# Reading a unit's two PSUM score tiles with one maximum and one exp of 1024 columns in a two-layer attention and FFN kernel

## The reference

```python
x = L0_attn_x                                    # (16, 512, 128)
xn = _layernorm(x); x = x + attn0(xn) + ffn0(xn) # 16 heads of 64, causal, ALiBi slopes
xn = _layernorm(x)
# second attention (attn1), H = 8, D = 8
q1, q2 = q[..., 0, :], q[..., 1, :]              # after rotary; k the same
def sdpa(q, k, v):
    scores = jnp.einsum('bshd,bthd->bhst', q, k) * d ** (-0.25)
    w = jax.nn.softmax(scores, axis=-1)
    return jnp.einsum('bhst,bthd->bshd', w, v)
o = sdpa(q1, k1, vfull) - lam * sdpa(q2, k2, vfull)
o = (o * rsqrt(mean(o * o) + 1e-8) * ln_w + ln_b) * (1 - LAMBDA_INIT)
x = x + o.reshape(b, s, e) @ Wo.T + ffn1(xn)
```

## Time and profile before

| | |
|---|---|
| runs, us | 2466.5, 2472.6, 2473.2; median 2472.6 |
| profiled execution | 2475.1 us, its span on the engines 2473.2 us |
| mean granted TensorE clock | 0.982 |
| PE matmuls / DVE / ACT / POOL busy | 2349.1 / 1832.7 / 1876.5 / 1443.5 us |
| maxima L1362 | 1024, 679 ns each |
| exps L1044 | 1024, 607 ns each |

### The profile page before, as it was taken

One profiled execution on the slowest core, in us unless ns is written; L12 is line 12 of the kernel. 1 busy time (PEld: TensorE's weight loads), 2 busy tenths in 40 slices (PEclk: granted clock), 3 DMA queues, 4 the chain that ended last, 5 costly groups with the idle time before them and its releaser, 6 DMA issues.

```text
span 2473.2 us, 82166 instructions
## 1 busy us (share of the span) xinstructions
PE 2349.1 (95%) x32896; PEld 1136.1 (46%) x32896; DVE 1832.7 (74%) x5637; ACT 1876.5 (76%) x4707; POOL 1443.5 (58%) x1356
## 2 busy tenths in 40 slices
PE   6999999999999999999999999999999999999877
PEld 3554444444544444444444544444444444544322
DVE  5568687787877778687787877778786887877674
ACT  4877877877778787877878777887777877787434
POOL 5975574756648466574756657475574756556201
PEclk9999999999999999999999999999999999999877
DMA  3011020200202020020201102020020201102020
GB/s 100 4 38 23 7 58 3 57 6 20 45 3 62 3 57 8 6 58 3 62 3 29 36 7 57 3 57 7 7 58 3 62 2 40 25 3 57 2 56 5
DMA packets 59946, 70.45 MB, mean 28 GB/s; under 512 B 11056, under 2 KB 55344, under 8 KB 56368
## 3 DMA queue, kind: packets, MB, share of 16 engines
q1 hardware_dynamic: 59568, 65.21, 11.4%
HBM read 35.04 MB, written 29.36 MB: 26 GB/s over the span
## 4 chain that ended last, share of the span: by engine, by line
PE 77%; DVE 16%; ACT 3%; issue 2%; DMA 1%; SPq 0%; POOL 0%; POOLq 0%; DVEq 0%; ACTq 0%
PE pj L1595 18%; PE pj L1691 12%; PE sc L1659 10%; PE pj L1721 10%; PE sc L1676 5%; PE sc L1768 5%; PE pj L1707 5%; DVE mx L1362 5%; PE pj L1615 5%; PE sc L1754 4%; DVE pq L1309 4%; PE pj L1585 3%; ACT pt L1044 1%; DVE y L1330 1%; DVE onrm L1372 1%
## 5 line engine op out<-in xcount | busy, mean ns | idle before, releaser
L845 POOL TENSOR_SCALAR pq<-pq,rsum 128x128 f32<-128x128 f32 (+3 forms) x1024 | 1151.8, 1139 | 772.8 <-DVE rsum L1316 771.2
L1362 DVE TENSOR_REDUCE mx<-sc 128x1 f32<-128x512 f32 x1024 | 644.1, 679 | 247.5 <-PE sc L1768 247.1
L996 ACT ACTIVATE pq<-pq,mx 128x128 f32<-128x128 f32 (+3 forms) x1024 | 569.8, 570 | 25.9 <-DVE mx L1309 25.7
L1044 ACT ACTIVATE pt<-sc 128x512 f32<-128x512 f32 x1024 | 543.9, 607 | 36.0 <-PE sc L1754 34.6
L1309 DVE CUSTOM_DVE_ANT_0 pq<-sc,relkey 128x128 f32<-128x128 f32 (+3 forms) x1024 | 448.5, 484 | 158.7 <-PE sc L1659 156.1
L1014 ACT ACTIVATE pt<-sc 128x512 f32<-128x512 f32 (+1 forms) x768 | 376.6, 535 | 162.3 <-PE sc L1676 159.5
L1659 PE MATMUL sc<-K,Q 64*128 64x128 f32 (+3 forms) x2048 | 362.5, 452 | 15.7 <-DVE mx L1309 9.4
L1691 PE MATMUL pj<-pt,v 128*32 128x512 f32 (+3 forms) x4096 | 303.8, 437 | 8.5 <-DVE y L1330 5.7
L1676 PEld LDWEIGHTS sc<-ident,pq 64*128 64x128 f32 x5120 | 200.1, 138 | 189.8 <-issue 99.7
L1595 PE MATMUL pj<-xnT,wqkv 128*32 128x512 f32 x2048 | 263.1, 606 | 4.0 <-ACT xnT L947 2.0
L1676 PE MATMUL sc<-ident,pq 64*128 64x64 f32 x5120 | 234.6, 227 | 7.4 <-DVE mx L1309 4.0
(11 more groups left out here) (117 smaller groups left out, 2836.7 us busy)
## 6 DMA issues: line engine op xcount, KB each, us to landing
scr_p<-y SPq DMA_DIRECT2D x160, 128.0 KB, 2.4
QS<-scr_p SPq DMA_DIRECT2D x30, 384.0 KB, 5.8
KS<-scr_p SPq DMA_DIRECT2D x30, 384.0 KB, 8.5
x_in<-in_L_attn_x SPq DMA_DIRECT2D x16, 256.0 KB, 2.9
scr_p<-tanh SPq DMA_DIRECT2D x32, 128.0 KB, 2.4
out_x<-xres SPq DMA_DIRECT2D x15, 256.0 KB, 2.3
QS<-nrow SPq DMA_DIRECT2D x180, 4.0 KB
wqkv<-in_L_attn_w_qkv SPq DMA_DIRECT2D x1, 1536.0 KB, 6.5
```

The costliest lines, as they stand in the source:

```text
L845: pool.tensor_scalar(rows, rows, rsum[:, row_slot(i, p), c:c + 1], None, ALU.mult).then_inc(s_scl, 1)
L996: act.activation(rows, rows, ACT.Exp, scale=-1.0, bias=mx0[:, row_slot(i, p), c:c + 1], accum_out=lsum[:, row_slot(i, p), c:c + 1]).then_i ...
L1044: act.activation(pt1[:, 2 * (unit % UNITS) + h, :], sc[tile_bank(i, "st1", 2 * n + h)][:, :], ACT.Exp, scale=float(DS) ** -0.25).then_inc( ...
L1362: dve.reduce_max(mx1[:, g % 2, at:at + 1], sc[tile_bank(i, "mx1", 2 * t + h)][:, :], AXIS.X).then_inc(s_mxd1, 1)
```

## The change

The six score banks are allocated as three PSUM tensors of two neighbouring banks each, and `sc[n]` becomes a view of one half, so all other users stay as they are. `row_max1` waits once for both tiles and takes both maxima with one instruction over a 128x2x512 source, writing two columns of `mx1` that lie 8 apart; it adds 2 to its semaphore at its end. `exp1` waits once for both tiles and writes both slots of `pt1` with one instruction, adding 2. The numbers of matmuls, their order and every other step are the same.

```diff
-        sc = [ps(f"sc{n}") for n in range(SCB)]
+        sc_pairs = [ctx.enter_context(nc.psum_tensor(f"sc{n}", [P, 2, T], F32)) for n in range(SCB // 2)]
+        sc = [sc_pairs[n // 2][:, n % 2, :] for n in range(SCB)]
...
-                for h in range(2):
-                    act.wait_ge(s_st1, i.upto(L1N, 2 * n + h + 1))
-                    act.activation(pt1[:, 2 * (unit % UNITS) + h, :], sc[tile_bank(i, "st1", 2 * n + h)][:, :],
-                                   ACT.Exp, scale=float(DS) ** -0.25).then_inc(s_exp1, 1)
+                act.wait_ge(s_st1, i.upto(L1N, 2 * n + 2))
+                both = tile_bank(i, "st1", 2 * n)
+                assert both % 2 == 0 and tile_bank(i, "st1", 2 * n + 1) == both + 1
+                slot = 2 * (unit % UNITS)
+                act.activation(pt1[:, slot:slot + 2, :], sc_pairs[both // 2][:, :, :], ACT.Exp, scale=float(DS) ** -0.25).then_inc(s_exp1, 2)
...
-                for h in range(2):
-                    at = 2 * NT * h + n
-                    dve.wait_ge(s_mxf1, i.upto(L1N, 2 * t + h + 1))
-                    dve.reduce_max(mx1[:, g % 2, at:at + 1], sc[tile_bank(i, "mx1", 2 * t + h)][:, :], AXIS.X).then_inc(s_mxd1, 1)
+                dve.wait_ge(s_mxf1, i.upto(L1N, 2 * t + 2))
+                both = tile_bank(i, "mx1", 2 * t)
+                assert both % 2 == 0 and tile_bank(i, "mx1", 2 * t + 1) == both + 1
+                dve.reduce_max(mx1[:, g % 2, n:n + 2 * NT + 1:2 * NT], sc_pairs[both // 2][:, :, :], AXIS.X).then_inc(s_mxd1, 2)
```

## The result

| | before | after |
|---|---|---|
| median of 7 runs each, us | 2473.2 (2466.5 to 2481.9) | 2489.6 (2483.4 to 2490.8) |
| profiled execution / its span | 2475.1 / 2473.2 | 2489.4 / 2487.6 |
| distance from batch to batch, steady state | 147.46 | 148.08 |
| maximum / exp, ns each | 679 and 679 / 607 and 607 | 1217 / 1025 |

The kernel got slower: the ratio of the runs is 1.005, 95% interval 1.0034 to 1.0067, which is 8 to 17 us. The forecast was 2474.3 with a range up to 2485; it is outside. (One correction to the text ahead of it: a batch has 32 units, which are 64 tiles. No term of the sum uses the wrong number.)

A forecast was written before the change was run, and what follows sets the result against it. TensorE (PE), 97% busy, was taken to bound the kernel. Per period +2x0.26-0.33 = +0.19, 14 periods +2.7, tail -1.0: total +1.7 us, so the median 2472.6 becomes 2474.3; range 2463 to 2485, the forecast's own 2470 to 2480.

The forecast's parts named there:

- rivals 2 and 4: Wide instructions: 2, the whole start is saved, 2463 us, chance 0.10; 4, nothing is saved, 2485 us, chance 0.11.
- the sum of the whole start: With 0.15 and 0.18 us saved per pair: loss 28x0.10 = 2.8, gain 14x0.65 = 9.1, tail 3, giving 2463.
- The gains on the chain: Savings of wide maxima and exps that reach the chain in one steady-state period: 0.33 us together.
- term (b): DVE near 1426.7 to 1431.28 us: three maximum pairs' savings reach the chain, 0.21 less 0.01, so 0.20 us per period.
- Term (a): The maximum pair at 1323.66 us opens a DVE run on the chain lasting to 1330; saves 0.07 us per period.
- (c): The exp pair at 1445.33 us is on the chain and holds an L1754; saves 0.06 us per period.
- The pattern: Twice per period, 28 times, DVE starts pair two on a half-filled pair; after the change it starts 0.49 us later.
- PE loses 0.26: Per pattern, the k projection's weight loads wait for the residual sum L1285 and start at 1310.78 instead of 1310.52 us.
- rival 3: At DVE's pair two of the pattern, PE loses the full 0.42 us; tail adds 4; 2484 us, chance 0.13.
- its own signs: Forecast wrong if wide instructions last near 1.28 and 1.08, k projection starts on time, or period leaves 147.7 by over 0.3.
- The tail: Last two batches, behind about 2290 us: maxima save 1.2 and exps 0.9, late second tiles cost 1.1; total -1.0 us.
- late second tiles: In the tail, about ten starts wait for a second tile not yet filled, few on the chain; cost +1.1 us.

The follow-up runs named there:

- four units by tile: After, but the maxima of units 14, 15, 27 and 28 of each batch are read tile by tile; ratio to before 0.9978, period 147.09 us.
- maxima alone: Maxima wide as in after, exps tile by tile as in before; ratio to before 1.0056, period 148.09 us.
- the kernel that adds 1: After, but each wide maximum and exp adds 1 instead of 2 and waits count units; ratio to before 1.0034, period 147.84 us.
- joint wait: Before with narrow maxima, but DVE waits for both tiles before the first, banks released one by one; ratio to before 1.0069, period 148.42 us.
- four units by tile with adds of 1: After with units 14, 15, 27, 28 read tile by tile and adds of 1 instead of 2; ratio to before 0.9976, period 146.95 us.
- exps alone: Exps wide as in after, maxima tile by tile as in before; ratio to before 1.0004, period 147.46 us.
- joint release: Before with narrow maxima, but both banks are released by the second reduce, adding 1 per unit; ratio to before 1.0068, period 148.31 us.
- narrow adding 2: Before, but each narrow maximum adds 2 to its semaphore and thresholds are doubled; ratio to before 1.0015, period 147.60 us.

## Why the prediction was wrong, point by point

**What bounds the kernel: right.** PE is the bound, DVE and ACT have slack, and neither's saved busy time came out as such: DVE's fell by 29 us and ACT's by 22.5 over the span. That PE's would stay the same was wrong, it fell by 42 with the matmuls side by side and the kernel still got slower.

**The sizes of the wide instructions: right.** 1217 and 1025 ns against 1.21 and 1.02 us; rivals 2 and 4 (whole start saved, nothing saved) fall with them. (The 0.65 in the sum of the whole start isn't worked out there; the three terms at 0.15 and 0.18 add up to at most 0.78, which would make it 2461. The forecast doesn't use it.) In a run of two, DVE takes 2.36 us for the wide ones, which is 1.14 from start to start against 1.20 for a narrow pair: 0.06 saved, forecast 0.07:

```profile
1304.31 2.36 DVE L1364 TENSOR_REDUCE mx<-sc 128x2 f32<-128x1024 f32 x2
...
1315.07 1.95 ACT L1047 ACTIVATE pt<-sc 128x1024 f32<-128x1024 f32 x2
```

The estimate by the Trainium skill (VectorE: DVE Perf Modes, "The TRN2 errata — SBUF-src ops pay a fixed extra latency per instruction") was 0.125 for DVE, twice what the row shows, and 0.14 for ACT. ACT's pace does agree with that: 1.95-1.02 = 0.93 from start to start, where four narrow ones in 2.21 us make 1.07 per pair. It brought nothing, since exps don't set the time.

**The gains on the chain: right in sum, wrong in part.** Forecast 0.33 per period; four units by tile shows 0.37. But the maxima give all of it. In the trace with maxima alone PE gains 0.14 at the L1769 behind 1391 us of before (medians over the 13 periods) and 0.25 near 1431, and loses 0.04 and 0.06 to separate waits at 1327 and 1433. These and some 0.07 at two smaller places make 0.36. So term (b), 0.20, is there (0.25 less the 0.06 behind it). Term (a), 0.07, is not: where it should have come PE loses 0.04, and gains only 0.03 in the kernel that adds 1. The 0.14 at 1391, which the forecast missed, made up for (a) and (c): the sum came out right by luck. Term (c), 0.06 for the exp, failed too: it was on the chain, but the next thing PE waits for, a maximum, was as late as before.

**The pattern: mechanism, places and count right, price wrong.** This is the step that failed: "PE loses 0.26", which measured 0.49. It took L1285 as 0.42 late, and it was 0.66 (it ends 3.94 us instead of 3.28 behind the start of the same L1676 matmul). The missing 0.24 on DVE are, by the raw start and end times: 2x0.07 for the separate wait, once at each pair (shown by the kernel that adds 1); 2x0.03 because a reduce that waits for the second of two matmuls running side by side starts 0.07 behind it, and one that waits for the first 0.04 (joint wait: 0.07 for its first pair too); and 2x0.02 because the two wide reduces here took 1.23 us, not the mean of 1.21. 0.17 us of slack in front of the k projection turn 0.66 into 0.49. DVE's slack behind the pattern was enough, as the forecast said: rival 3 (PE loses all that DVE loses) is not what happened, though its time, 2484, came nearer than the forecast's. By its own signs the forecast was wrong too: the period left 147.7 by 0.38, more than the 0.3 allowed.

Why it was missed: the forecast costed the waits "at nothing" because one in two disappears. It looked at when the awaited tile is ready, not at what form the wait has, and it gives the diff's `then_inc(..., 2)` no price. The error was doubled by the position: pair one's late start delays its release, the refill, and pair two's start.

**The sum of the steady state.** Forecast 14x(2x0.26-0.33) = +2.7. Measured 14x(2x0.49-0.36) = 8.7, with 0.36 what maxima alone gave, beside 14x0.62 from the periods and 9.2 from the averages of three executions.

**The tail: forecast -1.0, measured +0.7 to +5.2, 3.1 more than before on average.** The chain of the kernel after, 2299 to 2394 us, then 2394 to 2488:

```profile
by line: PE pj L1723 21.3%; PE pj L1709 9.9%; PE pj L1693 9.2%; DVE mx L1364 9.1%; PE pj L1597 5.9%; issue 5.8%; PE sc L1770 4.3%; ACT pt L1047 3.7%; PE sc L1756 3.6%; PE pj L1587 2.5%; PE sc L1678 1.9%; POOL rms L855 1.7%; DMA QS<-nrow 1.6
...
by line: PE pj L1723 21.8%; issue 13.1%; DVE mx L1364 12.2%; ACT pt L1047 8.4%; PE sc L1756 7.2%; PE pj L1597 5.2%; PE sc L1770 5.1%; PE pj L1617 3.9%; PE pj L1587 1.9%; ACT oraw L1022 1.9%; POOLq L515 1.8%; ACT y L965 1.7%; DMA pq<-nrow 1.
```

In the tail's first 95 us the maxima's line is 9.1% of the chain, where it was 14.3% (so the cheaper maxima may count there), but in the last 94 us 12.2%, where it was 7.0%. It is tempting to see more waits in the second share, but the two traces laid over each other say that little is lost in that part. Nearly all of it is lost at one place, the 30 us of work that before does from 2280 to 2310 us. The stretches view of before, then of the same work in the kernel after:

```profile
2280.20:2310.17 29.97, 24.79 (x326) 11.69 (x326) 21.85 (x44) 16.29 (x36) 10.12 (x7) 0.94 0.01 2
...
2291.91:2324.85 32.94, 25.71 (x327) 11.96 (x326) 20.93 (x29) 15.89 (x28) 10.12 (x7) 0.79 0.01 2
```

It takes 3.0 us longer, at a granted clock of 0.79 instead of 0.94. This holds for all 14 profiles of this study, by the time at half clock within this work:

| at half clock, us | profiles | longer by, us |
|---|---|---|
| 3.7 to 4.6 | before (3), four units by tile with adds of 1 | -0.2 to +0.3 |
| 7.1 to 7.2 | after (3rd), both wide with adds of 1, four units by tile | +0.3 to +0.8 |
| 11.1 to 11.3 | exps alone, joint release | +2.6 to +3.2 |
| 13.8 to 17.0 | after (1st, 2nd), maxima alone, narrow adding 2, joint wait | +3.0 to +4.2 |

Behind it the rest of the tail differs from the first profile of before by -0.9 to +1.1 us in all of them. The three executions of after average +2.7 in the 30 us and +0.2 in the rest, those of before +0.1 and -0.4. So 2.5 of the 3.1 us come from this one place, and 0.6 from all that follows, which is less than what executions of one kernel differ by there (1.3 for after). Exps alone and narrow maxima that add 2 have the loss though their steady part hardly changed, and the latter has no wide instruction at all, so it doesn't need the late second tiles that the forecast priced at +1.1. The forecast had no term for the clock, and its own terms (2.1 saved, 1.1 lost) are too small to be told from what executions differ by: they are neither shown nor refuted. That the loss goes with the clock is shown; what tips the clock there is not, nor how often it does so in either kernel, since apart from before and after each was profiled once.

## What to carry to other kernels

Merging two tiles into one instruction joins two waits and two releases; before counting the saved start, look in the timeline for places where the reader begins on the first tile while the second is being filled, since each of them cost about a fill here (0.36 to 0.49 us, a fill takes 0.39), and keep those few tile by tile. Keep the count that an instruction adds to its semaphore at 1 by counting in the merged unit. And where a faster engine's work is on the chain, ask what the bound engine waits for next: if that is another engine's work, the gain can be handed back.

## What the runs showed of the hardware that was not expected

- A reduce on DVE that adds 2 to its semaphore does not take its own wait along: an instruction of 21 ns for the wait appears (none in the kernels that add 1; one for each such reduce, 448, 512 or 1024, in those that add 2), and the start behind the awaited matmul moves from 0.03 to 0.10 us, or from 0.07 to 0.14 for the wide one. For the few wide exps that ACT had waited for, adds of 2 against 1 make 0.15 against 0.13. The Trainium skill (Perfetto Trace Analysis, "Identifying Dependency Chains") tells of such instructions only for waits on several engines; here the wait for one semaphore got one. It also has compute semaphores count by 1 (Trainium Kernel Development and Optimization, "Key Constraints"): the runs with adds of 2 show that 2 works, at this price.
- The first of two matmuls that run side by side is usable for a reader 0.03 to 0.04 us behind its end, the second 0.07 (1024 narrow maxima of before, 512 wide ones that add 1; medians of those that DVE had waited for).
- TensorE's granted clock in the last 200 us: 0.80 in all three executions of before, 0.77, 0.76 and 0.79 in those of after. One kernel's executions can differ there: after had 7.1, 14.1 and 16.2 us at the lower of two levels (1.2 GHz) within the same 30 us of work, and took 0.8, 3.0 and 4.2 us longer than before.
